# Attention scores in full banks, and the exponentials moved into the tick of their scores

## What is computed

```python
q = q * cos + rotate_half(q) * sin
k = k * cos + rotate_half(k) * sin
scale = HEAD_DIM ** (-0.5)
scores = jnp.einsum('bhqd,bhkd->bhqk', q, k) * scale
...
scores = jnp.where(causal, -jnp.inf, scores)
attn = jax.nn.softmax(scores, axis=-1)
out = jnp.einsum('bhqk,bhkd->bhqd', attn, v)
```

## Time and profile before

| | |
|---|---|
| time, three runs | 3060.85, 3074.97, 3075.13 us, median 3074.97 |
| profiled execution | 3059.91 us, of which the span of instructions 3058.1 us |
| busy: TensorE, its weight loads, VectorE, ScalarE, GpSimd | 2735.0, 1735.1, 1885.7, 1213.5, 749.8 us |
| mean granted TensorE clock | 0.922 of 2.4 GHz |
| first pass: 1536 matmuls (L735), 1024 masked and 512 plain reductions | 632.1, 501.5, 351.8 us |
| second pass: 1536 matmuls (L749), 1536 exponentials, 3072 value matmuls | 535.6, 674.7, 360.2 us |

### The profile page before, as it was taken

One profiled execution on the slowest core, in us unless ns is written; L12 is line 12 of the kernel. 1 busy time (PEld: TensorE's weight loads), 2 busy tenths in 40 slices (PEclk: granted clock), 3 DMA queues, 4 the chain that ended last, 5 costly groups with the idle time before them and its releaser, 6 DMA issues.

```text
span 3058.1 us, 45977 instructions
## 1 busy us (share of the span) xinstructions
PE 2735.0 (89%) x15374; PEld 1735.1 (57%) x15374; DVE 1885.7 (62%) x5534; ACT 1213.5 (40%) x2706; POOL 749.8 (25%) x1279
## 2 busy tenths in 40 slices
PE   4885899899998999899998999989998999989996
PEld 3663566456655666466655566566664666555544
DVE  5443666665667556666667666675566666666652
ACT  1321244454434444444434343343444444343352
POOL 2321232223222222213322232222322133221111
PEclk7986899999999999899899999999999999999998
DMA  2024103311232213411134112332134111343211
GB/s 58 1 62 112 22 17 95 95 40 40 59 102 74 53 25 95 122 40 39 40 86 123 39 37 61 87 89 52 26 86 120 47 42 36 83 116 78 58 36 45
DMA packets 137424, 193.99 MB, mean 63 GB/s; under 512 B 49439, under 2 KB 111214, under 8 KB 127854
## 3 DMA queue, kind: packets, MB, share of 16 engines
q1 hardware_dynamic: 131808, 190.89, 24.6%
q10 hardware_dynamic: 5390, 0.18, 0.1%
HBM read 122.34 MB, written 67.63 MB: 62 GB/s over the span
## 4 chain that ended last, share of the span: by engine, by line
PE 68%; DVE 15%; DMA 3%; issue 3%; ACT 2%; POOL 1%; SPq 1%; DVEq 0%; ACTq 0%; POOLq 0%
PE bank L735 10%; PE bank L768 8%; PE bank L749 8%; PE bank L664 4%; PE bank L571 4%; PE bank L502 3%; PE bank L551 3%; PE bank L678 3%; PE bank L511 3%; PE bank L520 3%; PE bank L665 3%; DVE bank L1087 3%; DVE mxa L1090 2%; PE bank L481 2%; PE bank L606 2%
## 5 line engine op out<-in xcount | busy, mean ns | idle before, releaser
L1290 ACT ACTIVATE pexp<-bank 128x512 f32<-128x512 f32 (+3 forms) x1536 | 674.7, 495 | 605.3 <-PE bank L749 603.6
L735 PE MATMUL bank<-stk,stq 128*128 128x512 f32 (+3 forms) x1536 | 632.1, 426 | 121.5 <-DVE mxa L1087 33.2
L1087 DVE CUSTOM_DVE_ANT_0 bank<-bank,maskneg 128x128 f32<-128x128 f32 (+3 forms) x1024 | 501.5, 497 | 376.8 <-PE bank L735 371.2
L735 PEld LDWEIGHTS bank<-stk,stq 128*128 128x128 f32 x1536 | 305.4, 201 | 502.1 <-issue 449.7
L749 PE MATMUL bank<-stq,stk 128*128 128x512 f32 (+3 forms) x1536 | 535.6, 422 | 55.3 <-ACT pexp L1290 51.3
L1090 DVE TENSOR_REDUCE mxa<-bank 128x1 f32<-128x512 f32 x512 | 351.8, 687 | 159.7 <-PE bank L735 154.1
L1438 POOL TENSOR_SCALAR_AFFINE_SELECT pexp<-pexp 128x256 f32<-128x256 f32 x512 | 211.6, 419 | 786.9 <-ACT pexp L1290 786.8
L749 PEld LDWEIGHTS bank<-stq,stk 128*128 128x128 f32 x1536 | 281.2, 202 | 196.7 <-ACT pexp L1290 121.6
L768 PE MATMUL bank<-pexp,vsm 128*32 128x512 f32 (+3 forms) x3072 | 360.2, 543 | 8.1 <-POOL pexp L1438 7.7
L1356 POOL TENSOR_SCALAR_AFFINE_SELECT arena<-arena 128x512 f32<-128x512 f32 x128 | 79.4, 644 | 411.2 <-ACT arena L1194 411.2
L571 PE MATMUL bank<-arena 32*128 32x256 f32 x1024 | 155.6, 423 | 15.6 <-DVE arena L895 11.1
(11 more groups left out here) (183 smaller groups left out, 4170.7 us busy)
## 6 DMA issues: line engine op xcount, KB each, us to landing
stq<-q_halves SPq DMA_DIRECT2D x128, 256.0 KB
arena<-rope_table SPq DMA_DIRECT2D x8, 2048.0 KB
q_halves<-arena SPq DMA_DIRECT2D x32, 512.0 KB, 2.9
k_halves<-arena SPq DMA_DIRECT2D x32, 512.0 KB, 2.8
stk<-k_halves SPq DMA_DIRECT2D x64, 256.0 KB
stk<-k_halves SPq DMA_DIRECT2D x128, 128.0 KB
v_rows<-arena SPq DMA_DIRECT2D x16, 544.0 KB, 4.1
vsm<-v_rows SPq DMA_DIRECT2D x16, 544.0 KB, 3.8
```

The lines of the kernel that those rows point to most:

```text
L735: mm(bk[:, 0:k1 - k0], stq[b_][:, h % 2, qb * P:(qb + 1) * P], stk[b_][:, h % 2, k0:k1], start=True, stop=True).then_inc(s["r_full"], 1)
L1087: nc.vector.tensor_tensor_reduce(out=sc, in0=sc, in1=maskneg[:, CH - (k1 - k0):CH], scale=1.0, scalar=LOWEST, op0=ALU.add, op1=ALU.max, ac ...
L1290: nc.scalar.activation(pexp[:, u % NPX, j, 0:n], ps(j)[:, 0:n], ACT.Exp, scale=DK ** -0.5).then_inc(s["exp_done"], 1)
```

## The change

Part by part:

- **Packing.** `packs` puts the twelve blocks of a head into nine units of exactly 512 columns each: three units hold two blocks side by side in one bank (128 and 384, 256 and 256, 128 and 384 columns), six hold one. The matmuls and the reductions are the same ones, 1536 each in all; the wait is before a unit's first matmul and the signal behind its last, on both engines. A group has 36 units, and 1152 in all in place of 1536.
- **Their place.** Three units in two core ticks: one in part 0 of the first tick, then one in part 0 and one in part 1 of the second. The first of these ticks is the one that has `values` in part 1, the second has none. The ticks at which a head begins and ends, the maxima are transposed (`max_tr_at`) and the operands loaded (`load_at`) come out the same as before.
- **Exponentials.** ScalarE takes those of the unit whose scores TensorE makes in the same core tick, j = 0 in part 1 (between the steps of stream 0 and stream 1) and j = 1 in part 2 (behind the step of stream 1, ahead of the tail's).
- **GpSimd's masking** of a unit is one core tick earlier.

```diff
-        sunits = [(h, qb, k0, min(P * (qb + 1), k0 + CH)) for h in range(G) for qb in range(NT)
-                  for k0 in range(0, P * (qb + 1), CH)]
+        packs = (((0, 0), (2, 0)), ((3, 0),), ((1, 0), (5, CH)), ((4, 0),), ((4, CH), (6, CH)), ((5, 0),), ((6, 0),), ((7, 0),),
+                 ((7, CH),))
+        sunits = []
+        for h in range(G):
+            for pack in packs:
+                col, blocks = 0, []
+                for qb, k0 in pack:
+                    n = min(P * (qb + 1), k0 + CH) - k0
+                    blocks.append((qb, k0, n, col))
+                    col += n
+                sunits.append((h, blocks))
...
-            score_at[SX - LEAD + n // 2, n % 2] = divmod(n, NSU)
-        max_tr_at = {SX - LEAD + NSU // 2 * (g + 1) + 1: g for g in range(NG * NB)}
+            score_at[SX - LEAD + n // 3 * 2 + (n % 3 + 1) // 2, n % 3 // 2] = divmod(n, NSU)
+        max_tr_at = {SX - LEAD + NTU * (g + 1) + 1: g for g in range(NG * NB)}
...
                 def score(g, i):
-                    h, qb, k0, k1 = sunits[i]
+                    h, blocks = sunits[i]
...
-                    mm(bk[:, 0:k1 - k0], stq[b_][:, h % 2, qb * P:(qb + 1) * P], stk[b_][:, h % 2, k0:k1],
-                       start=True, stop=True).then_inc(s["r_full"], 1)
+                    for qb, k0, n, col in blocks:
+                        last = mm(bk[:, col:col + n], stq[b_][:, h % 2, qb * P:(qb + 1) * P], stk[b_][:, h % 2, k0:k0 + n],
+                                  start=True, stop=True)
+                    last.then_inc(s["r_full"], 1)
...
                 def core_dve(t, part):
...
-                        if k1 == P * (qb + 1):
-                            nc.vector.tensor_tensor_reduce(out=sc, in0=sc, in1=maskneg[:, CH - (k1 - k0):CH], scale=1.0, scalar=LOWEST,
-                                                           op0=ALU.add, op1=ALU.max, accum_out=dst).then_inc(s["r_used"], 1)
-                        else:
-                            nc.vector.reduce_max(dst, sc, AX).then_inc(s["r_used"], 1)
+                        for qb, k0, n, col in blocks:
+                            dst = mxa[:, g % 2, NT * h + qb:NT * h + qb + 1] if k0 == 0 else mxb[:, g % 2, 4 * h + qb - 4:4 * h + qb - 3]
+                            sc = r_bank("s", g, i)[:, col:col + n]
+                            if k0 + n == P * (qb + 1):
+                                last = nc.vector.tensor_tensor_reduce(out=sc, in0=sc, in1=maskneg[:, CH - n:CH], scale=1.0, scalar=LOWEST,
+                                                                      op0=ALU.add, op1=ALU.max, accum_out=dst)
+                            else:
+                                last = nc.vector.reduce_max(dst, sc, AX)
+                        last.then_inc(s["r_used"], 1)
...
                 def core_act(t, part):
-                    u = t - SX
-                    if part == 0 and 0 <= u < NU * NB:
-                        g, i = divmod(u, NTU)
-                        c, kb, hp = tunits[i]
+                    u = t - SX + 1
+                    if part and 0 <= u < NU * NB:
+                        c, kb, hp = tunits[u % NTU]
                         n = width(c, kb)
+                        j = part - 1
                         if u >= NPX:
                             nc.scalar.wait_ge(s["pv_done"], (u - NPX) // 2 + 1)
-                        for j in range(2):
-                            nc.scalar.wait_ge(s["t_ps"], 2 * u + j + 1)
-                            nc.scalar.activation(pexp[:, u % NPX, j, 0:n], ps(j)[:, 0:n], ACT.Exp, scale=DK ** -0.5).then_inc(s["exp_done"], 1)
+                        nc.scalar.wait_ge(s["t_ps"], 2 * u + j + 1)
+                        nc.scalar.activation(pexp[:, u % NPX, j, 0:n], ps(j)[:, 0:n], ACT.Exp, scale=DK ** -0.5).then_inc(s["exp_done"], 1)
...
                 def core_pool(t, part):
-                    u = t - SX - 1
+                    u = t - SX
...
-                    at = SX - LEAD + n * NSU // 4 - 4
+                    at = SX - LEAD + n * NTU // 2 - 4
```

More of the change, by code:

```diff
@@ L1081, in core_dve @@
                         g, i = score_at[t, part]
-                        h, qb, k0, k1 = sunits[i]
-                        dst = mxa[:, g % 2, NT * h + qb:NT * h + qb + 1] if k0 == 0 else mxb[:, g % 2, 4 * h + qb - 4:4 * h + qb - 3]
+                        h, blocks = sunits[i]
                         r_filled(nc.vector, "s", g, i)
-                        sc = r_bank("s", g, i)[:, 0:k1 - k0]
-                        if k1 == P * (qb + 1):
-                            nc.vector.tensor_tensor_reduce(out=sc, in0=sc, in1=maskneg[:, CH - (k1 - k0):CH], scale=1.0, scalar=LOWEST,
-                                                           op0=ALU.add, op1=ALU.max, accum_out=dst).then_inc(s["r_used"], 1)
-                        else:
-                            nc.vector.reduce_max(dst, sc, AX).then_inc(s["r_used"], 1)
+                        for qb, k0, n, col in blocks:
[7 more added lines that the diff above has]
+                        last.then_inc(s["r_used"], 1)
                         if i == NSU - 1:
```

## The result

The changed kernel takes 3034.3 us, the median of four runs from 3031.85 to 3040.39; the kernel before took 3070.43 us in four runs beside it (3060.85 to 3075.13). The ratio is 0.9889, 95% interval 0.9858 to 0.9921: 34 us faster, where 90 to 95 were forecast. The profiled execution took 3035.41 us, with a span of 3033.7.

The account below looks back on a forecast made before the run. TensorE's stream bounds the kernel. Removed waits of 80 + 45 us, times 0.7, minus 15 for front banks, plus 24 for clock, minus 7 for transfers, give 90 us: 2970, written as 2975 us, range 2880 to 3085.

Parts of the forecast that it names:

- the first-pass wait that was to go: TensorE's first-pass scores waiting for VectorE's reductions: 80 us removed, the recorded wait falling from 82 to 20 to 40.
- the price of the front's banks: Front matmuls on TensorE get one of three banks later, behind ScalarE's delayed copies: 15 us cost, ends 0 and 160.
- times 0.7: Share of the 125 us of removed TensorE waits counted as staying, since the late engine is still late: 88 us.
- a part 1 unit of a double tick: Score unit on TensorE said to wait only for the single unit, reduced first in VectorE's tick; three of four places loosened.
- Its own example: TensorE idles 1.21 us behind VectorE's front statistics and a reduction; the 128-column block was taken as a part 1 unit.
- "does not do what it says" rival: VectorE's dense stretches outlast any lead of a unit; some 10 us of each wait go, 3045 to 3075; chance 0.14.
- The clock: A fifth of 477 us at 1.2 GHz goes: 24 us gain, ends 0 and 50; mean clock 0.93 to 0.95.
- 31 us of gain: Transposed scores on TensorE wait less for ScalarE's exponentials: 45 us, ends 20 and 85, before the 0.7.
- "slower" rival: ScalarE loses its lead and the front's three banks stall TensorE, from about 0.25 us in 460 ticks; chance 0.16.
- 7 for transfers: Deduction for more exposed transfers of the tail, which do not shrink with the tick: 7 us.
- The masking wait: GpSimd's earlier masking takes away waits of a few microseconds, counted within the exponentials' term.
- Splitting the pairs: Separating ScalarE's paired exponentials costs next to nothing: two together 1.18 us or less, one alone 0.59 us.

Follow-up runs that it names:

- pack_only: The changed kernel with exponentials and masking as in the kernel before, so the packing and its places alone: 0.9859 of before, 3026.43 us.
- pack_wait: The packing alone, with a unit's two already fulfilled waits repeated ahead of each bank's second block: 0.9846 of the kernel before.
- pack_sig: The packing alone, with an extra signal that nobody waits for behind the first block of each pair: 0.9847 of the kernel before.
- pack_swap: The packing alone, with the double ticks moved to those that have value matmuls: 0.9804 of the kernel before.
- adjacent: The kernel before, unpacked, with both score units of a tick in part 0, one right behind the other: 1.0036 of the kernel before.
- places_unpacked: The packing alone's order, places and pairs, but each block with its own bank, wait and signal: 1.0316 of the kernel before.
- exp_both_p1: The changed kernel with both exponentials in part 1, ahead of stream 1's step: 0.9972 of the kernel before.
- exp_only: The kernel before, unpacked, with only the moved exponentials and the earlier masking: 1.0014 of the kernel before.
- exp_both_p2: The changed kernel with both exponentials in part 2, behind stream 1's step: 0.9804 of the kernel before.
- newton1: The changed kernel with two of three refinement steps left out of the linear attention's reciprocal square roots: 0.9787 of the kernel before.
- newton1_before: The kernel before with two of three refinement steps left out of the reciprocal square roots: 0.9913 of the kernel before.

## Why the prediction was half right

The direction was right and the time lies in the range; the gain was forecast at 90 us and came to 34 to 36. That the range held is in part luck: the larger part of the gain, the packing's, did not come where the prediction's steps put it. Two steps failed: the first-pass wait that was to go, and the price of the front's banks.

**The packing: the removed wait is the step that failed.** 80 us of waits, times 0.7, was to give 56 us, with the first-pass waits at "20 to 40" us. They are 78.6 us in pack_only and 89.5 after, against 82.2 before: nothing of the 80 us shows. They are fewer and longer. pack_only still gains 43 us, so the size is near, but where it comes from is open.
The prediction said that a part 1 unit of a double tick waits only for the single unit "which VectorE does first in this tick, ahead of its front step", and so is loosened. The timeline of the kernel after shows why it need not be:

```profile
1864.10 1.39 DVE L814 BATCH_NORM_STATS2 stats<-x 128x6 f32<-128x256 f32 x4
...
1867.79 1.42 DVE L823 TENSOR_SCALAR arena<-x,mv,rstd 128x256 f32<-128x256 f32 x4
...
1869.13 0.28 DVE L1099 CUSTOM_DVE_ANT_0 bank<-bank,maskneg 128x128 f32<-128x128 f32 x1
...
1869.34 0.59 DVE L1099 CUSTOM_DVE_ANT_0 bank<-bank,maskneg 128x384 f32<-128x384 f32 x1
...
1870.13 0.47 PE L745 MATMUL bank<-stk,stq 128*128 128x256 f32 x2 [1.85 <-DVE mxa L1099]
```

The single unit, 128 and 384 columns, has its scores from TensorE at 1867.15 (from 1866.63, 0.52 us). It is first in VectorE's tick, but VectorE comes to it only at 1869.13. It has had no idle time since 1862.57: 1.39 us of statistics, the two reductions of the tick before (0.66 and 0.69 us) and 1.42 us of normalisation stand ahead. TensorE's part 1 unit at 1870.13 idles 1.85 us for it. The prediction counted what stands ahead of a reduction within a tick, and not that VectorE can be most of a tick behind.
Its own example had this case and was read wrongly. The block of 128 columns in the earlier trace rows is not the sixth of its head: VectorE reduces it next of this width, and writes its maximum to `mxa`, where the sixth block's goes to `mxb`.

```profile
1879.84 0.29 DVE L1087 CUSTOM_DVE_ANT_0 bank<-bank,maskneg 128x128 f32<-128x128 f32 x1
1880.05 0.14 DVE L1087 DVE_READ_ACCUMULATOR2_ANT mxa<- 128x1 f32 x1
```

So it is the first block of a head, a part 0 unit, whose place the packing leaves as tight as it was. This is the argument of the "does not do what it says" rival, dense stretches longer than any lead. It was true of these waits, yet the kernel gained.

Where the 43 us are is only partly settled. They are not in signals or waits as such (pack_wait, pack_sig), nor does their place in ticks without value matmuls explain them (pack_swap). Closeness of matmuls gives nothing with the old ring (adjacent), but was not tried with the lead held equal. The capacity of the bank is needed in these places (places_unpacked). The busy time of the score matmuls fell from 632.1 to 506.6 us, but it did so in adjacent as well, and there it is worth nothing. What counts is TensorE as a whole: before to after its recorded idle time rose by 25 us, and its busy time, whose ends are modelled, fell by 49. So the gain stands in no row of waits; it is in stalls inside modelled ends, in faster matmuls, or in both.

**The clock: a term that may hold.** The prediction added 24 us for it. Half-clock time fell by 64 us in the traces, and the mean of 0.932 is within the forecast 0.93 to 0.95. The executions on record allow an estimate of what goes with the clock. The kernel before ran 67 times in the experiments, with 3056 to 3091 us at clocks of 0.926 to 0.914, and by a straight line through them 0.001 of clock goes with 2.6 us (2.1 over all kernels). pack_only's mean clock is 0.930 and after's 0.934, against 0.920. By these slopes 21 to 27 us of the packing's gain, and 28 to 36 us of the 36 of the whole change, go with the clock. It does not show which is the cause, for a wait less also changes when TensorE is busy. Nor does the clock rank kernels: exp_both_p1's is as high as pack_only's, at 36 us more. But it means that the 43 us, which have their share of the clock in them, are to be held against more than 56.

**The exponentials: the front banks are the term that was mis-sized.** The prediction had 31 us of gain and 15 of cost, net 16; measured is -9 us (after against pack_only), or -4 without the packing, neither of them clear of noise. The cost is the term "72 x 0.2 = 15 us" for the front's banks. In time it is 26 us for one exponential ahead of stream 1's step, and 51 for two; with both behind it the move gives 17 to 20 us. The mechanism was foreseen: stream 1 takes two banks in a tick, and the next front product waits for one. In rows the size is right as well, 9 us of waits before and 25 after. What was missed is that in time it costs about twice what the rows show. It is the mechanism of the "slower" rival too, at some 0.06 us in each of 460 ticks and not the 0.25 from which it decides. The gain is smaller than 31 us too, and the rows show a part of the reason: what TensorE gains at ScalarE comes back at VectorE. Summed over all its rows, TensorE waits for VectorE 163 us before, 177 in pack_only, 196 in exp_only, 208 after and 210 in exp_both_p2, and L580's wait for L906 alone doubled from 15.1 in pack_only to 31.7. The factor of 0.7 took 38 us off for this, and in the rows it is 44. That VectorE is late is seen in the timeline above; that work taken from it pays is shown by newton1 and newton1_before, with 31 and 27 us.

By the measured parts, the packing is 13 us under its 56 and the exponentials 25 under their 16. The 24 for the clock less 7 for transfers have no measurement of their own, as a part measured alone has both in it; without them the sum is 34, the measured gain.

**What held.** The masking wait fell as said (L779 for GpSimd, from 7.7 to 0.4 us). Splitting the pairs cost ScalarE next to nothing, as said: the exponentials' busy time rose from 674.7 to 697.2 us and that of the engine fell from 1213.5 to 1209.3. But the remark that the pair of the earlier trace rows shows no overlap does not hold for pairs at large: 1536 exponentials of 0.495 us in the mean are 760 us and keep ScalarE busy for 674.7, an overlap of 0.11 us in each pair. That the later reduction of a bank's first block costs nothing was not tried by itself, and no run reads a bank while a matmul writes it; VectorE still waits 306.0 us at L1099 and 126.4 us at L1102 for these matmuls, so it is early in many ticks, as it was. Waits ahead of L796 and L802 were to stay near 19 and rose to 28.6. VectorE's busy time did not rise. From one sequence's transfer of `x_rows` to the next, a full stretch of 120 ticks, the chain takes 350 to 354 us, down from 358 to 359, not the 347 forecast.

**Open.** How the packing's 43 us divide between stalls hidden in modelled ends, the clock and the order; and why, of 25 us for each exponential ahead of stream 1, only 11 to 14 stand in TensorE's rows.

## What to carry to other kernels

On an engine that works in order, put an instruction that depends on work of the same tick behind those that free banks for the busiest engine: ahead of them it takes away the lead that hid them, and this can cost more than the wait that it shortens. Before you forecast that a wait goes, ask whether the late engine is behind by less than the added lead; where it is most of a tick behind, the wait comes back at another unit. When a wait is put down to a tile of shared memory, read in the source which semaphore is waited for. Do not take the busy time of one group for the gain: it falls when matmuls of that group stand side by side, in a slower kernel too. When a change's parts are independent in the code, measure each alone and in more than one place: the best version here had the same two ideas in other places.

## What the hardware showed unexpectedly

GpSimd's power grows with its columns: 128x4 takes 1043 ns and 128x64 takes 10771 ns, some 0.16 us for each further column by these two. 384 more signals, or as many pairs of waits that are already met, cost TensorE nothing that can be measured. And VectorE, busy for 61% of the span, still counts: 23 to 28 us taken from it at one place gave 27 to 31.
